# The order of the output pieces and of VectorE's product in a layer pair on one TensorE-bound core

## The reference

```python
# layer 0
scale = cond @ norm_w.T + 1.0
h = x * (scale[:, None, :] * rsqrt(mean(x * x) + EPS))
val, gate = split(h @ up_w.T, 2)
h = val * gelu(gate)
x = act_quant(h) @ weight_quant(down_w).T + x
# layer 1
x = x + a_alpha * attention(ada_rmsnorm(x, t, ...), W_q, W_k, W_v, W_o)   # 16 heads of 16
f_alpha = (t @ ffn_alpha_w.T)[:, None, :]
n = ada_rmsnorm(x, t, ffn_gamma_w, ffn_beta_w)
x = x + f_alpha * (silu(n @ gate_w.T) * (n @ hidden_w.T) @ out_w.T + out_b)
```

## Time and profile before

| | us |
|---|---|
| median of 3 runs | 1012.45 |
| lowest and highest | 1010.81, 1016.49 |
| profiled execution, its own time | 1006.49 |
| its span, first to last instruction | 1004.7 |
| PE busy | 960.3 (96%) |
| VectorE busy | 729.3 (73%) |
| ScalarE busy | 552.9 (55%) |
| POOL busy | 273.4 (27%) |

### The profile page before, as it was taken

One profiled execution on the slowest core, in us unless ns is written; L12 is line 12 of the kernel. 1 busy time (PEld: TensorE's weight loads), 2 busy tenths in 40 slices (PEclk: granted clock), 3 DMA queues, 4 the chain that ended last, 5 costly groups with the idle time before them and its releaser, 6 DMA issues.

```text
span 1004.7 us, 18048 instructions
## 1 busy us (share of the span) xinstructions
PE 960.3 (96%) x6636; PEld 640.8 (64%) x6636; DVE 729.3 (73%) x1215; ACT 552.9 (55%) x1162; POOL 273.4 (27%) x262
## 2 busy tenths in 40 slices
PE   6999999999999998999899899989998999999998
PEld 4777777776545656656665575556656656655577
DVE  4988788998787785778477667857785777667254
ACT  5566455453766654565365546645653655465432
POOL 1365523222101321132222312221322222133142
PEclk9999999999999999999999999999999999999899
DMA  9635566434421130223034012302130230210000
GB/s 284 169 97 146 130 148 133 117 96 89 131 71 64 55 70 2 86 69 54 12 100 97 2 59 80 70 2 85 59 65 12 101 74 3 83 35 8 1 27 22
DMA packets 93751, 75.60 MB, mean 75 GB/s; under 512 B 44880, under 2 KB 79768, under 8 KB 93664
## 3 DMA queue, kind: packets, MB, share of 16 engines
q1 hardware_dynamic: 81880, 61.91, 23.0%
q10 hardware_dynamic: 11784, 12.54, 4.9%
HBM read 27.73 MB, written 12.61 MB: 40 GB/s over the span
## 4 chain that ended last, share of the span: by engine, by line
PE 77%; DVE 11%; ACT 4%; issue 2%; POOL 2%; SPq 2%; DMA 1%; ACTq 0%; DVEq 0%; POOLq 0%
PE bank L423 14%; PE bank L1081 11%; PE bank L1322 10%; PE bank L1062 8%; PE bank L1403 7%; PE raw_pair L979 5%; PE bank L881 4%; DVE rowmax L1012 3%; PE bank L1332 3%; PE bank L940 2%; PE bank L1144 2%; PE bank L1348 2%; PE bank L333 2%; DVE amax L486 1%; PE bank L1391 1%
## 5 line engine op out<-in xcount | busy, mean ns | idle before, releaser
L1070 ACT ACTIVATE probs<-bank 128x512 f32<-128x512 f32 x512 | 278.8, 598 | 246.6 <-PE bank L1062 246.0
L1012 DVE TENSOR_REDUCE rowmax<-raw_pair 128x2 f32<-128x1024 f32 x225 | 275.0, 1222 | 109.9 <-PE raw_pair L979 109.0
L423 PE MATMUL bank<-up_w,xs_part 128*128 128x512 f32 x768 | 192.0, 404 | 3.8 <-POOL xs_part L405 3.8
L1062 PE MATMUL bank<-q_stack,k_stack 50*128 50x512 f32 x480 | 175.2, 420 | 5.5 <-DMA q_stack<-shift_rows 3.9
L423 PEld LDWEIGHTS bank<-up_w,xs_part 128*128 128x128 f32 x768 | 143.1, 191 | 37.4 <-POOL xs_part L405 4.5
L1378 POOL TENSOR_TENSOR hid<-scratch,hid 128x512 fp32r<-128x512 f32 x64 | 81.8, 1279 | 232.1 <-ACT hid L1374 232.1
L979 PE MATMUL raw_pair<-k_stack,q_stack 48*128 48x512 f32 x440 | 136.1, 445 | 1.5 <-DVE rowmax L1012 1.5
L1081 PE MATMUL bank<-probs,v_ext 128*17 128x512 f32 x1024 | 135.7, 602 | 0.6
L1062 PEld LDWEIGHTS bank<-q_stack,k_stack 50*128 50x128 f32 x480 | 82.6, 187 | 45.2 <-ACT probs L1070 25.0
L1403 PEld LDWEIGHTS bank<-out_w,hid 64*128 64x128 f32 x1152 | 84.0, 191 | 37.8 <-issue 34.8
L1403 PE MATMUL bank<-out_w,hid 64*128 64x256 f32 x1152 | 90.1, 286 | 14.3 <-POOL hid L1378 14.2
(11 more groups left out here) (210 smaller groups left out, 1659.1 us busy)
## 6 DMA issues: line engine op xcount, KB each, us to landing
q_stack<-split SPq DMA_DIRECT2D x48, 128.0 KB, 2.9
q_stack<-hid SPq DMA_DIRECT2D x42, 128.0 KB, 2.9
k_stack<-hid SPq DMA_DIRECT2D x42, 128.0 KB, 2.9
xk<-xT SPq DMA_DIRECT2D x32, 128.0 KB, 3.0
xt<-x_tok SPq DMA_DIRECT2D x32, 128.0 KB, 2.7
x_spill<-x1t ACTq DMA_DIRECT2D x32, 128.0 KB, 2.5
xa_spill<-xa ACTq DMA_DIRECT2D x32, 128.0 KB, 2.4
x_in<-xa_spill SPq DMA_DIRECT2D x8, 512.0 KB, 5.2
```

Of the source, the lines that this page charges most:

```text
L423: last = nc.tensor.matmul(bank[j][:], xs_part[a][:, m % 2, k, :], up_w[w][:, k, col + j * W:col + (j + 1) * W], start=(i == 0), stop=(i == ...
L1012: nc.vector.reduce_max(rowmax[:, e:e + RAWS + 1:RAWS], raw_pair[:], AX.X).then_inc(raw_read, 1)
L1062: nc.tensor.matmul(score_bank[c % 2][:], k_rows[rows, slot, kt * P:(kt + 1) * P], q_rows[rows, slot, :], start=True, stop=True).then_inc(s ...
L1070: nc.scalar.activation(probs[:, (kt % 2) * J + j, :], score_bank[c % 2][:], ACT.Exp).then_inc(exp_done, 1)
```

## The change

The order of the eight output pieces puts the four tiles' first parts ahead of their second parts. So two tiles are open in a bank at the same time, and only the first matmul of a bank's first tile carries `start`; the second tile's first matmul writes without it. On VectorE the product is issued behind the maximum (and behind the shift, if one is due in that step) instead of ahead of it.

```diff
         def out_half_pe(c, t, i, step, rows):
             a, wp, f = step
             return nc.tensor.matmul(ab[t // HALF][:, (t % HALF) * D:(t % HALF + 1) * D],
                                     hid[a][rows, f, t * P:(t + 1) * P], out_w[wp][rows, f, :],
-                                    start=(rows == LOWER and i == 0), stop=(rows == UPPER and i == len(PARTS) * NH - 1))
+                                    start=(rows == LOWER and i == 0 and t % HALF == 0),
+                                    stop=(rows == UPPER and i == len(PARTS) * NH - 1), skip_group_check=True)
...
-        OUT_PIECES = ((0, 0), (2, 0), (0, 1), (2, 1), (1, 0), (3, 0), (1, 1), (3, 1))
+        OUT_PIECES = ((0, 0), (2, 0), (1, 0), (3, 0), (0, 1), (2, 1), (1, 1), (3, 1))
...
             for h in range(HALVES + 1):
...
                         if p[1] == T - 1:
                             x2_dve(dve, b - 1, 1, u + at["wo"][1])
-                    elif p[0] == "hidden":
-                        product_dve(dve, b - 1, p[1], u + at["hidden"])
                     elif p[0] == "out" and p[1] % HALF == HALF - 1 and p[2] == 1:
...
                 for p in done:
                     if p[0] == "gate":
                         gate_dve(dve, b - 1, p[1])
+                    elif p[0] == "hidden":
+                        product_dve(dve, b - 1, p[1], u + at["hidden"])
                     elif p == ("qk", 1, 1):
```

## The result

| us | before | changed |
|---|---|---|
| median | 1013.63 (4 runs, 1010.81 to 1016.49) | 965.03 (4 runs, 964.71 to 965.74) |
| ratio, 95% interval | | 0.9521, 0.9492 to 0.9551 |
| profiled execution | 1006.49 | 964.71 |
| its span | 1004.7 | 962.9 |

The account below looks back on a forecast made before the run. It took PE's waits, for POOL's low part of `hid` and VectorE's maximum, as the bound. Gains of 17.4 and 18.0 us sum to 35.4, taking the median from 1012.45 to 977.0, range 967 to 997.

Parts of the forecast that it names:

- the distance to the median: Whole kernel: the median stays 6.0 us above the profiled execution, so 971 becomes 977.0.
- Part 1: Output pieces reordered: step 26's stall for POOL's low part gone in batches 1 to 5, plus clock; 17.4 us.
- Part 2: VectorE's product behind the maximum, odd steps 11 to 25: 2.5 us a batch, 18.0 us with batch 7.
- rival 2: Steps 12 and 20: L1018 and the next shift operation each meet a POOL operation; 2 us a batch, 989; chance 0.15.
- Batch 7: Shift some 2.3 us sooner, 1.6 counting, with three clean steps and step 20: about 3.0 us gain.
- ScalarE's (1): ScalarE uses up the 0.45 us cover on exps, PE's scores wait; Part 2 gives nothing, 995; chance 0.17.
- the slower one (3): The hid copy holds ScalarE's queue, exps 1.05 us late, 0.6 lost a pair of steps: 1029; chance 0.03.
- (4): Last hid block late for step 28 too, Part 2 gives nothing, Part 1 gives 4.5: 1008; chance 0.05.

Follow-up runs that it names:

- the pieces alone: Changed kernel with the product put back ahead of the maximum, so only the output pieces' order differs from the kernel before: 991.54 us, ratio 0.9818.
- the fills: Kernel before with dummy matmuls where PE idles: in step 26 of batches 1 to 5, 1005.72 us; also in batch 7's steps 16 and 24, 1001.81 us.
- the version with batch 7 alone: Kernel before with the product behind maximum and shift in batch 7 only: 1001.13 us, ratio 0.9915.

## Why the prediction missed

It forecast the right direction and mechanisms for batches 1 to 6, and missed the range by 2 us through two terms. The forecast of 977.0 is 12.0 above the measured 965.0: 6.4 of these are the first term, nearly all in batch 7, and 5.7 the second, the distance to the median.

- **Part 1** (17.4): right in mechanism and size. By the profiles batches 1 to 5 got 17.0 us shorter with the pieces alone, with the stall gone and nothing waiting at step 28. That the median fell by exactly 17.4 is luck, since its interval is 14.7 to 21.9. L1378 ended 6.0 after step 26's start, as worked out, and the piece started 0.9 later.
- **Part 2 in batches 1 to 6** (2.5 a batch): right. Batch 6 gained 2.6; the even steps last 3.26 (forecast 3.27), the maximum starts at 0.71 (0.72), steps 20 and 21 take 5.29 (5.12 and 0.1 to 0.2 of stall), and L1018 meets POOL as priced: 0.55 us, from 369.17 to 369.72, while POOL's L1378 ends at 369.69, the gate behind the shift. The Trainium skill's page "SBUF — State Buffer", section "Who interferes with whom", has the rule that the prediction weighed: the second of the two to issue waits for the whole of the first. By that rule, the trace agrees again. The second collision with L1123 (rival 2) did not come, since L1123 runs at 370.38, after the shift. In part the sum came out right because two errors met: the seven even steps gave 1.9 us and not 1.5, since 14 and 22 last only 3.10, and step 19, which was priced at nothing, lost 0.3 to ScalarE.
- **Batch 7** ("about 3.0 (bounds 0 and 5)"): this is the first step that failed; it was 9.5. The forecast priced the clock in batches 1 and 2 and put it at nothing where the trace of before showed most of it, in batch 7 (0.88 and 0.66 in the windows above): 4.5 us by the fills. And the waits gave about 5 and not 3.0, for two reasons. The first is one assumption: "the two transfers that ScalarE issues stand behind its later exps, so 1.6 of it counts". The timeline of the changed kernel in batch 7, at step 14:

```profile
872.09 0.62 ACTq L1030 DMA_DIRECT2D q_stack<-shift_rows  x1
...
872.90 1.07 ACT L1070 ACTIVATE probs<-bank 128x512 f32<-128x512 f32 x2
```

ScalarE's queue issued its first transfer at 872.09 and its second at 872.74, ahead of the exps' execution at 872.90 that stand before them in the program; the last of SP's six went at 874.38, so ScalarE's were not the late ones. Step 16 starts 7.39 us after step 13 instead of 10.07: 2.7, not 1.6, though 0.2 of it is step 14's, which the forecast counted apart. The second reason is a wait that was priced at nothing, the one for the next shift's rows ahead of step 24, longer than the one in the earlier trace rows. The kernel before:

```profile
935.51 0.49 PE L1062 MATMUL bank<-q_stack,k_stack 50*128 50x512 f32 x2 [2.10 <-DMA q_stack<-shift_rows]
```

From step 22 to step 24 the changed kernel takes 5.50 us and the kernel before 6.77, 1.3 less. The rest, 0.9, is in steps 12, 18 and 20.
- **The distance to the median** ("I keep that distance", 6.0): the second step that failed; it was 0.3 in the changed kernel. A part of the 6.0 was the draw of three runs: the 43 runs of the kernel before in the experiments have a median of 1009.05, 2.6 above the profiled execution. The rest goes with the clock. The profiled execution of before had a mean granted clock of 0.990. The 43 runs have 0.978 to 0.991, and their times follow it (the median time of the runs at each clock):

```
clock   0.991    0.990    0.988    0.986    0.985    0.983    0.981    0.980    0.978
us      1004.52  1006.46  1007.36  1009.05  1011.52  1010.84  1013.86  1014.92  1016.22
runs    1        7        8        11       3        2        6        4        1
```

A line through all 43 runs falls by 8.5 us for each 0.01 of clock (correlation -0.93), and drawn on to 1.000, where no run lies, it meets 997.5. The changed kernel has 0.996 to 0.998 in its four runs and a spread of 1 us, where the groups of the kernel before spread over 6 to 11. That the clock makes a part of the difference, and does not only go with it, is shown by the fills, which shortened nothing else. The stalls let the clock fall in some executions and not in others: in the profiled one of before in batches 1, 2 and 7, in that of the version with batch 7 alone, whose batches 1 to 5 are those of before, in batches 1, 2 and 3. The median holds more of it than the profiled run did. A forecast from one profile that removes such stalls has to allow for the clock at each of them, and not only where it happened to fall.
- **Rivals.** ScalarE's (1) did not come in the ordinary pairs, with about 0.5 us to spare, but its mechanism is there in step 19 of each batch 1 to 6, for 0.3 us; the slower one (3) did not come. Collisions (2) came once a shift in steps 12 and 20, at the price of the forecast, and the time was given back in steps 14 and 22. The double collision that rival 2 feared stood in the kernel before, in batch 7: L1020, behind L1018 of the earlier trace rows, took 1.21 us at 904.62 beside POOL and takes 0.18 in the changed kernel. (4) did not come.

## What to carry to other kernels

An idle stretch of the tensor engine can cost more than its length, by an amount that differs from run to run: look at the granted clock of several runs, and count it for each stretch that a change removes. When two edits touch the same chain, price each with the other absent; here one made the other's stall longer and was worth 11.6 us alone and 26.5 on top (991.5 to 965.0). And where a ring (raw matmuls, maximum, raw matmuls) is what bounds a pair of steps, an edit that shortens the first step without shortening the ring gives the time back in the second.

## What was not expected of the hardware

- Dummy matmuls in idle stretches made the kernel before 7.2 us faster, though the waits that they stand in were not shortened: the clock stayed at 2.4 GHz there, and the 24 matmuls of a piece take 1.65 us there against 2.93 at 1.2 GHz.
- A DMA in ScalarE's program was issued before earlier operations of the same engine had run (872.09 against 872.90 to 873.97), so here the transfer was not late because ScalarE's computing was. The other way round it costs: in step 18 ScalarE stood idle for 0.73 us while its queue issued two transfers ahead of the tanh.
- A stall of 4.22 us was followed by the low clock in all five places, those of 2.8 to 2.9 us in two of five in one profile and in three of five in another, and the one of 0.97 us was not.
